# Routed experts of a six-stage kernel: the mask of the two best by replacing them, and the padding cleared behind the router's subtraction

## The chip, the cores and the metric

The kernel runs on one core of a Trainium2 chip. The metric is the device time of one execution in microseconds (us): three runs of the kernel before took 3339.98 to 3342.47 us, with a median of 3340.1. The core's engines work side by side, each through its own queue in order, and meet only at semaphores: TensorE (PE, with its weight load PEld), VectorE (DVE), ScalarE (ACT), GpSimd (POOL), and SyncE (SP), which issues the DMAs here.

## The reference

x has 16 sequences of 256 tokens with 128 channels. Six blocks are added to it one after another. The change touches two of them, the first and the third, which are the same routed FFN with the same weights (the others are a retention layer, two attention-and-expert layers and a plain attention). Cut to the routed FFN:

```python
def _L0_ffn_ref(x, rW1, rb1, rW2, rb2, rW3, rb3, eW1, eb1, eW2, eb2):
    capacity = int(T / E * CAPACITY_FACTOR)                  # 40 slots of each of 8 experts
    h = jax.nn.relu(x @ rW1 + rb1)                           # 128 -> 512
    h = jax.nn.relu(h @ rW2 + rb2)                           # 512 -> 512
    scales = jax.nn.softmax(h @ rW3 + rb3, axis=-1)          # 512 -> 8
    topk_scales, topk_experts = jax.lax.top_k(scales, k)     # the two best of 8
    onehot = jax.nn.one_hot(e_flat, E, dtype=jnp.int32)
    pos_excl = jnp.cumsum(onehot, axis=1) - onehot           # place of a token among its expert's
    keep = pos < capacity
    ...                                                      # tokens to slots, two layers per expert
    out = jnp.sum(topk_scales[..., None] * gathered, axis=2)
x = x + 0.5 * _L0_ffn_ref(_layernorm(x, axis=-1), ...)
```

## The kernel before, in words

`routed_ffn` is called twice. It splits the 32 tiles of 128 tokens into G = 8 groups of GT = 4 tiles, and runs over steps s = 0 to 10. Each engine has its own loop over s, and the order of the work in it is written out by hand. In step s the router works on group s (`layer1`, `layer2`, `partial`, `logits`), the mask, the counting and the slots work on group s - 1 (`count`, `slots`, `turn_weights`), and the experts on an earlier pair of groups (`hidden`, `output`, `turn_slots`, `back`). The engines hand their results over through PSUM banks in four rings of two: `ra` (emptied by ScalarE) and `rv` (emptied by VectorE) for the router, `ea` and `ev` likewise for the experts.

The router's products are made in three parts, of a high and a low part of both factors (`split_product`, L221 to L223). So every h1 chunk goes through two engines: ScalarE (chunks 0 and 2) or VectorE (chunks 1 and 3, `route_hidden`, L573 and L576) takes it from PSUM as high part and as whole, and GpSimd subtracts one from the other for the low part (`rest_of_h1`, L783). TensorE starts layer 2 only when all four low parts are there. The low part of x comes from GpSimd too (L777). The weights' high parts are written by ScalarE (L487), their low parts by VectorE (L689), both in the first FFN only: in the second, `w.load` is None and they are there already.

The experts' slots are found like this, on VectorE: `softmax_divide` (L590 to L596) makes the scores `sc`, 8 for each token; `pick` takes the eight largest in order (`max`, L603) and the places of these (`max_index`, L608) and casts the first two places to float (L611); `mark` compares the numbers 0 to 7 with each of the two (L616), adds the results to the mask (L620), a 1 at the two best experts of each token, and makes an offset of it (L622). `memset(k.idle)` writes a scratch element. TensorE counts with the mask (`count`, L270 and L271), and `place` turns the counts into a 0/1 matrix `d` (L628, L633), which TensorE multiplies with.

Padding: the weighting matrices `gts` and the experts' transposed outputs `eos` fill 80 of the 96 partitions that the products of `back` read, so rows 64 to 95 of four tiles are cleared once at the start of each FFN, by VectorE (L683, each 32 x 2048). Two of these tiles lie in a buffer named all_qs. ScalarE waits for the clears (`padded`) only in step 1, before anything is written to the tiles.

In the profile the names of both FFNs begin with f_: f_ra and f_rv are the router's rings, f_h_hi and f_h_lo the parts of h1, l_rw_hi and l_rw_lo those of the router's weights.

Of the kernel before, what the change touches and what calls it, by code (L numbers as in the profile page):

```python
# [22 lines left out]
U32 = mybir.dt.uint32  # L23
ALU = mybir.AluOpType
# [3 lines left out]
P = 128  # L28
# [4 lines left out]
E0, HID, CAP = 8, 512, 40  # L33
# [4 lines left out]
ROWS = 96  # L38
# [83 lines left out]
def routed_ffn(nc, tag, x_sb, k, w):  # L122

    G, GT, NB = B // 2, 4, 4
# [6 lines left out]
    with ExitStack() as ctx:  # L131
        a = Pool_(nc, ctx, tag)
# [8 lines left out]
        lp = a.sb("lp", [P, W])  # L141
        lg, ex, sc = [a.sb(n, [P, GT, E0]) for n in ("lg", "ex", "sc")]
        top, den = a.sb("top", [P, GT]), a.sb("den", [P, GT])
        best, best_at = a.sb("best", [P, GT, 8]), a.sb("best_at", [P, GT, 8], U32)
        best_f = a.sb("best_f", [P, GT, 2])
        eq = a.sb("eq", [P, GT, 2, E0])
        mask = a.sb("mask", [P, GT, E0], BF16)
        off, pos = a.sb("off", [P, GT, E0]), a.sb("pos", [P, GT, E0])
        d = a.sb("d", [P, GT * E0, CAP])
# [3 lines left out]
        eos, own = a.sb("eos", [ROWS, NB, NW, C]), a.sb("gts", [ROWS, GT, NW, P])  # L153
        stack = [k.qs[:, n, :, :].rearrange("p h t -> p (h t)").bitcast(F32) for n in range(2)]
        gts = [stack[0].rearrange("p (t v c) -> p t v c", t=GT, v=NW), own, stack[1].rearrange("p (t v c) -> p t v c", t=GT, v=NW)]
# [33 lines left out]
        def ring(name):  # L189
# [3 lines left out]

        ra, rv, ea, ev = ring("ra"), ring("rv"), ring("ea"), ring("ev")
        ra_taken, rv_taken, ea_taken, ev_taken = ra.emptied["x"], rv.emptied["h1"], ea.emptied["slots"], ev.emptied["slots"]
        (ln_stats, ln_aggr, ln_veps, ln_rstd, xn_ready, top_ready, lg_ready, ex_ready, den_step, sc_ready, best_step, bestf,
         mask_step, off_ready, d_ready, g_ready, padded, xt_ready, h1_ready, zeroed, ks_zeroed) = [a.sem(n) for n in (
             "ln_stats ln_aggr ln_veps ln_rstd xn_ready top_ready lg_ready ex_ready den_step sc_ready best_step bestf "
             "mask_step off_ready d_ready g_ready padded xt_ready h1_ready zeroed ks_zeroed").split()]
        block = ctx.enter_context(nc.Block())  # L200
        ROUTE = (ra, rv, ra, rv)
# [340 lines left out]
        def _(dve):  # L542
# [15 lines left out]
            def ln_apply(g):  # L558
                dve.wait_ge(ln_rstd, g + 1)
                if g >= 2:  # L560
                    EXPERT[1].full(dve, "slots", (g - 2, 1))
                for t in range(GT):
                    nc.vector.tensor_scalar(xn[:, g % 2, t, :], x_g[:, g, t, :], mv[:, t, 0:1], rstd[:, t:t + 1],
                                            ALU.subtract, ALU.mult).then_inc(xn_ready, 1)
# [34 lines left out]
            def pick(g):  # L599
                dve.wait_ge(sc_ready, g + 1)  # L600
                nc.vector.memset(k.idle, 0.0)
                for t in range(GT):
                    last = nc.vector.max(best[:, t, :], sc[:, t, :])  # L603
                last.then_inc(best_step, 1)
                dve.wait_ge(best_step, g * 2 + 1)
                nc.vector.memset(k.idle, 0.0)
                for t in range(GT):
                    last = nc.vector.max_index(best_at[:, t, :], best[:, t, :], sc[:, t, :])  # L608
                last.then_inc(best_step, 1)
                dve.wait_ge(best_step, g * 2 + 2)  # L610
                nc.vector.tensor_copy(best_f[:, :, :], best_at[:, :, 0:2]).then_inc(bestf, 1)  # L611

            def mark(g):
                dve.wait_ge(bestf, g * 2 + 1)
                for n in range(2):
                    last = nc.vector.tensor_tensor(eq[:, :, n, :], k.iota8.unsqueeze(1).to_broadcast([P, GT, E0]),  # L616
                                                   best_f[:, :, n:n + 1].to_broadcast([P, GT, E0]), ALU.is_equal)
                last.then_inc(bestf, 1)
                dve.wait_ge(bestf, g * 2 + 2)
                nc.vector.tensor_tensor(mask[:, :, :], eq[:, :, 0, :], eq[:, :, 1, :], ALU.add).then_inc(mask_step, 1)  # L620
                dve.wait_ge(mask_step, g + 1)
                nc.vector.tensor_scalar(off[:, :, :], mask[:, :, :], -1000.0, 1000.0, ALU.mult, ALU.add)\  # L622
                    .then_inc(off_ready, 1)
# [45 lines left out]
            def take_slots(q, b):  # L669
                ev.full(dve, "eos", (q, b))  # L670
                nc.vector.tensor_copy(eos[0:SW, b, :, :].rearrange("p v c -> p (v c)"), ev.bank("eos", (q, b))[0:SW, :])\
                    .then_inc(ev_taken, 1)
# [6 lines left out]
            dve.wait_ge(k.loaded, k.loaded_count)  # L679
            ln_measure(0)  # L680
            ln_apply(0)
            for n, tile in enumerate([eos] + gts):
                nc.vector.memset(tile[64:ROWS, :, :, :].rearrange("p b v c -> p (b v c)"), 0.0).then_inc(padded, 1)  # L683
            dve.wait_ge(w.router_loaded, w.router_count)
            if w.load is not None:
                for n, (lo, full, hi) in enumerate(((w.rw1_lo[:, :], w.rw1[:, :], w.rw1_hi[:, :]),
                                                    (w.rw2_lo[:, :, :], w.rw2[:, :, :], w.rw2_hi[:, :, :]))):
                    dve.wait_ge(w.router_hi_ready, n + 1)
                    nc.vector.tensor_tensor(lo, full, hi, ALU.subtract).then_inc(w.router_lo_ready, 1)  # L689
                nc.vector.memset(w.rw3[:, :, E0:32], 0.0)  # L690
                nc.vector.tensor_copy(w.rw3[:, :, 0:E0], w.rw3_in[:, :, :]).then_inc(w.rw3_ready, 1)
            for s in range(G + 3):
                group, q, e = s - 1, (s - 2) // 2, 4 * (s % 2)
                route, given, expert, closed = s < G, 0 <= group < G, 2 <= s < G + 2, s >= 4 and s % 2 == 0
                if route:
                    route_hidden(s, "h1", 1)
                    route_hidden(s, "h1", 3)
                if closed:
                    take_slots(q - 1, 1)
                    take_slots(q - 1, 3)  # L700
                if given:
                    softmax_divide(group)
                    pick(group)
                    mark(group)
                if s % 2:
                    if expert:
                        hidden(q, e)
                        hidden(q, e + 1)
                    if given:
                        place(group)  # L710
                    if s < G - 1:
                        ln_measure(s + 1)
                    if expert:
                        hidden(q, e + 2)
                        hidden(q, e + 3)
                    if route:
                        route_hidden(s, "h2", 1)
                    if given:
                        slots(group)
                    if s < G - 1:  # L720
                        ln_apply(s + 1)
                    if route:
                        route_hidden(s, "h2", 3)
                    if expert:
                        output(q, e // 2 + 1)
                else:
                    if closed:
                        residual(q - 1, 0)
                    if s == G + 2:
                        nc.vector.memset(stack[0][32:64, :], 0.0)  # L730
                    if given:
                        place(group)
                    if s < G - 1:
                        ln_measure(s + 1)
                    if route:
                        route_hidden(s, "h2", 1)
                    if closed:
                        residual(q - 1, 1)
                    if given:
                        slots(group)  # L740
                    if expert:
                        for n in range(4):
                            hidden(q, e + n)
                    if s < G - 1:
                        ln_apply(s + 1)
                    if route:
                        route_hidden(s, "h2", 3)
                    if expert:
                        output(q, e // 2 + 1)
                if given:  # L750
                    take_weights(group, 1)
                    take_weights(group, 3)
                if route:
                    softmax_shift(s)
                if s == 0:
                    dve.wait_ge(w.experts_loaded, w.experts_count)
                    if w.load is not None:
                        w.split_positions(dve)
# [1679 lines left out]
```

## Time and profile before

| what | value |
|---|---|
| median of 3 runs | 3340.1 us |
| the profiled execution | 3345.47 us |
| its span, first to last instruction | 3343.7 us |
| mean granted TensorE clock | 0.949 |
| busy: TensorE, VectorE, ScalarE, GpSimd | 87%, 66%, 59%, 59% |
| first routed FFN | from about 9 us to about 330 us |
| second routed FFN | from about 599 us to about 920 us |

The span is the part of an execution that the profile sees. The two routed FFNs are the stretches with names in f_. A row of a timeline gives a start in us from the span's first instruction, a duration in us, the engine, the line, the operation, what it writes and reads, how many instructions are merged in the row, and in brackets how long the engine was idle before it and what released it. Every row that is used stands in the section on rows below.

### The profile page before, as it was taken

How to read it: one execution, taken by the hardware profiler on the slowest of the kernel's cores; microseconds unless marked ns; L12 is line 12 of the kernel's file. 1: busy time of each engine (PE TensorE's matmuls, PEld its weight loads, DVE VectorE, ACT ScalarE, POOL GpSimd, SP SyncE). 2: the span in 40 equal slices, each digit the busy share in tenths (PEclk: the TensorE clock that was granted, in tenths of full speed). 3: DMA queues.
4: the chain of work that ended last, by engine and by line, in shares of the span. 5: the costliest groups of instructions: out<-in, count | busy, mean ns of one | idle time of the engine just before them, and what ended most of it. 6: DMA issues, size and time to landing. Idle time of an engine off the chain costs nothing. (4 is left out here: it accounts for less than half of the span.)

```text
span 3343.7 us, 68247 instructions
## 1 busy us (share of the span) xinstructions
PE 2921.0 (87%) x21536; PEld 2373.1 (71%) x21536; DVE 2221.2 (66%) x4993; ACT 1969.9 (59%) x5797; POOL 1963.2 (59%) x2223
## 2 busy tenths in 40 slices
PE   6899677699969899997999979995999999979998
PEld 4778555477857777775788856664777777758886
DVE  4544466454459999886555558885888998855554
ACT  2223233222348888886544459995888888844443
POOL 3223554322157777773999942221777777759998
PEclk9999889899979999998999989997999999989999
DMA  3000445000022211122555533331122111145554
GB/s 103 1 1 1 96 108 114 1 1 1 1 47 49 47 38 38 42 49 68 191 191 191 190 89 81 78 77 47 39 50 46 38 38 38 39 149 190 190 191 169
DMA packets 145439, 260.56 MB, mean 78 GB/s; under 512 B 13402, under 2 KB 118106, under 8 KB 122298
## 3 DMA queue, kind: packets, MB, share of 16 engines
q1 hardware_dynamic: 145210, 257.78, 26.7%
q8 instruction: 111, 1.82, 0.2%
q14 instruction: 118, 0.97, 0.1%
HBM read 204.06 MB, written 53.67 MB: 77 GB/s over the span
## 5 line engine op out<-in xcount | busy, mean ns | idle before, releaser
L2223 POOL TENSOR_TENSOR f4m_ht_lo<-f4m_ht,f4m_ht_hi 128x512 fp32r<-128x512 f32 x256 | 330.9, 1311 | 33.3 <-ACT f4m_ht_hi L2168 24.0
L2223 POOL TENSOR_TENSOR f6m_ht_lo<-f6m_ht,f6m_ht_hi 128x512 fp32r<-128x512 f32 x256 | 330.9, 1312 | 33.0 <-ACT f6m_ht_hi L2168 23.7
L2203 DVE SCALAR_TENSOR_TENSOR f4m_ht<-f4m_hr,f4m_gate 128x512 f32<-128x512 f32 x256 | 176.3, 691 | 168.3 <-PE f4m_hr L2099 159.7
L2203 DVE SCALAR_TENSOR_TENSOR f6m_ht<-f6m_hr,f6m_gate 128x512 f32<-128x512 f32 x256 | 176.3, 691 | 167.7 <-PE f6m_hr L2099 160.2
L1711 ACT ACTIVATE f4a_pr<-f4a_sr,f4a_nm 128x256 f32<-128x256 f32 x512 | 239.5, 480 | 60.4 <-DVE f4a_nm L1820 59.0
L2168 ACT ACTIVATE f4m_ht_hi<-f4m_ht 128x512 fp32r<-128x512 f32 x256 | 161.5, 632 | 191.7 <-DVE f4m_ht L2203 191.6
L2168 ACT ACTIVATE f6m_ht_hi<-f6m_ht 128x512 fp32r<-128x512 f32 x256 | 161.5, 632 | 191.5 <-DVE f6m_ht L2203 188.5
L1711 ACT ACTIVATE f6a_pr<-f6a_sr,f6a_nm 128x256 f32<-128x256 f32 x512 | 239.5, 480 | 54.1 <-DVE f6a_nm L1820 52.2
L1956 POOL TENSOR_TENSOR f6a_rr<-f6a_tmp 128x256 f32<-128x256 f32 x256 | 189.0, 738 | 137.2 <-DVE f6a_tmp L1828 136.9
L1956 POOL TENSOR_TENSOR f4a_rr<-f4a_tmp 128x256 f32<-128x256 f32 x256 | 189.1, 739 | 133.5 <-DVE f4a_tmp L1828 133.0
L1711 ACT ACTIVATE a_pr<-a_sr,a_nm 128x256 f32<-128x256 f32 x512 | 252.2, 553 | 10.3 <-DVE a_nm L1820 10.2
L1820 DVE TENSOR_REDUCE a_nm<-a_sr 128x2 f32<-128x512 f32 x256 | 173.4, 684 | 56.6 <-PE a_sr L1568 56.4
L1828 DVE TENSOR_TENSOR f6a_tmp<-f6a_ur,f6a_turn 128x512 f32<-128x512 f32 x256 | 175.2, 685 | 45.2 <-PE f6a_ur L1556 41.2
L1828 DVE TENSOR_TENSOR f4a_tmp<-f4a_ur,f4a_turn 128x512 f32<-128x512 f32 x256 | 175.1, 685 | 44.4 <-PE f4a_ur L1556 40.6
L1962 POOL TENSOR_TENSOR f4a_rr_lo<-f4a_rr,f4a_rr_hi 128x256 fp32r<-128x256 f32 x256 | 192.6, 752 | 1.5 <-ACT f4a_rr_hi L1767 1.5
L1962 POOL TENSOR_TENSOR f6a_rr_lo<-f6a_rr,f6a_rr_hi 128x256 fp32r<-128x256 f32 x256 | 192.5, 752 | 1.5 <-ACT f6a_rr_hi L1767 1.5
L1820 DVE TENSOR_REDUCE f6a_nm<-f6a_sr 128x2 f32<-128x512 f32 x256 | 175.2, 684 | 25.9 <-PE f6a_sr L1574 24.7
L1820 DVE TENSOR_REDUCE f4a_nm<-f4a_sr 128x2 f32<-128x512 f32 x256 | 175.1, 684 | 24.5 <-PE f4a_sr L1574 23.3
L1572 PE MATMUL f6a_sr<-f6a_pe_hi,f6a_rr_hi 128*128 128x256 f32 x512 | 190.2, 371 | 0.0
L1572 PE MATMUL f4a_sr<-f4a_pe_hi,f4a_rr_hi 128*128 128x256 f32 x512 | 189.0, 369 | 0.0
L1696 ACT ACTIVATE f6a_pts<-f6a_tr 128x512 f32<-128x512 f32 x256 | 155.3, 607 | 43.7 <-PE f6a_tr L1584 34.2
L1696 ACT ACTIVATE f4a_pts<-f4a_tr 128x512 f32<-128x512 f32 x256 | 155.5, 607 | 32.3 <-PE f4a_tr L1584 30.4
(423 smaller groups left out, 9905.3 us busy)
## 6 DMA issues: line engine op xcount, KB each, us to landing
f4m_gate<-f4m_gates SPq DMA_DIRECT2D x64, 1024.0 KB, 4.6
f6m_gate<-f6m_gates SPq DMA_DIRECT2D x64, 1024.0 KB, 4.7
r_scratch<-r_parts SPq DMA_DIRECT2D x32, 192.0 KB, 2.2
all_qs<-r_scratch SPq DMA_DIRECT2D x16, 384.0 KB, 4.7
all_ks<-r_scratch SPq DMA_DIRECT2D x16, 384.0 KB, 6.7
f4a_scratch<-f4a_parts SPq DMA_DIRECT2D x32, 192.0 KB, 2.1
all_qs<-f4a_scratch SPq DMA_DIRECT2D x16, 384.0 KB, 5.0
all_ks<-f4a_scratch SPq DMA_DIRECT2D x16, 384.0 KB, 6.7
```

What stands on the lines that cost most here:

```text
L1572: nc.tensor.matmul(out, rr_hi[at], pe_hi[:, :], start=False, stop=False)
L1696: return nc.scalar.activation(dst, src_, ACT.Copy)
L1711: last = nc.scalar.activation(pr[:, n % 4, x, :], sr.bank(b, n)[:, x * T:(x + 1) * T], ACT.Exp, bias=nm[:, n % SB, x:x + 1], accum_out=zs[ ...
L1820: nc.vector.tensor_reduce(nm[:, n % SB, :], sr.bank(b, n).rearrange("p (x s) -> p x s", x=2), AX.X, ALU.max, negate=True).then_inc(nm_read ...
L1828: nc.vector.tensor_tensor(tmp[:, hs % 2, :, :], ur.bank(b, hs).rearrange("p (u t) -> p u t", u=2), turn[:, :, :], ALU.mult).then_inc(ur.em ...
L1956: nc.gpsimd.tensor_tensor(rr[:, hs % RAW, :], tmp[:, hs % 2, 0, :], tmp[:, hs % 2, 1, :], ALU.add)\
L1962: nc.gpsimd.tensor_tensor(rr_lo[:, hs % RRS, :], rr[:, hs % RAW, :], rr_hi[:, hs % RRS, :], ALU.subtract)\
L2168: nc.scalar.activation(ht_hi[:, n % RB, :], ht[:, n % RB, :], ACT.Copy).then_inc(hi_ready, 1)
L2203: nc.vector.scalar_tensor_tensor(ht[:, n % RB, :], hr[:, n % HB, :], 0.0, gate[:, q % GB, n % LOADED, :], ALU.max, ALU.mult).then_inc(ht_r ...
L2223: nc.gpsimd.tensor_tensor(ht_lo[:, n % RB, :], ht[:, n % RB, :], ht_hi[:, n % RB, :], ALU.subtract)\
```

## The change

It has two parts. In `pick`, the eight largest scores stay, but places 2 to 7 of them are overwritten with -1.0, and `match_replace` copies the scores to `left` with the values that match one of the eight replaced by -1.0. Scores are positive, so what is below zero in `left` is one of the two best: `mark` makes the mask by one comparison. The cast, the two comparisons and the addition go, with the tiles `best_at`, `best_f` and `eq` and the semaphore `bestf`; a clear of 6 of 8 elements of `best` comes in, with its wait. In the VectorE queue of each routed FFN, the four clears of padding are moved behind the subtraction of the router's weights and what follows it.

```diff
@@ pick and mark @@
-                dve.wait_ge(best_step, g * 2 + 1)
+                dve.wait_ge(best_step, g * 3 + 1)
+                nc.vector.memset(best[:, :, 2:8], -1.0).then_inc(best_step, 1)
+                dve.wait_ge(best_step, g * 3 + 2)
                 nc.vector.memset(k.idle, 0.0)
                 for t in range(GT):
-                    last = nc.vector.max_index(best_at[:, t, :], best[:, t, :], sc[:, t, :])
+                    last = nc.vector.match_replace(left[:, t, :], best[:, t, :], sc[:, t, :], -1.0)
                 last.then_inc(best_step, 1)
-                dve.wait_ge(best_step, g * 2 + 2)
-                nc.vector.tensor_copy(best_f[:, :, :], best_at[:, :, 0:2]).then_inc(bestf, 1)
 
             def mark(g):
-                dve.wait_ge(bestf, g * 2 + 1)
-                for n in range(2):
-                    last = nc.vector.tensor_tensor(eq[:, :, n, :], k.iota8.unsqueeze(1).to_broadcast([P, GT, E0]),
-                                                   best_f[:, :, n:n + 1].to_broadcast([P, GT, E0]), ALU.is_equal)
-                last.then_inc(bestf, 1)
-                dve.wait_ge(bestf, g * 2 + 2)
-                nc.vector.tensor_tensor(mask[:, :, :], eq[:, :, 0, :], eq[:, :, 1, :], ALU.add).then_inc(mask_step, 1)
+                dve.wait_ge(best_step, g * 3 + 3)
+                nc.vector.tensor_scalar(mask[:, :, :], left[:, :, :], 0.0, None, ALU.is_lt).then_inc(mask_step, 1)
                 dve.wait_ge(mask_step, g + 1)
@@ the start of VectorE's program @@
             ln_measure(0)
             ln_apply(0)
-            for n, tile in enumerate([eos] + gts):
-                nc.vector.memset(tile[64:ROWS, :, :, :].rearrange("p b v c -> p (b v c)"), 0.0).then_inc(padded, 1)
             dve.wait_ge(w.router_loaded, w.router_count)
             if w.load is not None:
...
                 nc.vector.tensor_copy(w.rw3[:, :, 0:E0], w.rw3_in[:, :, :]).then_inc(w.rw3_ready, 1)
+            for n, tile in enumerate([eos] + gts):
+                nc.vector.memset(tile[64:ROWS, :, :, :].rearrange("p b v c -> p (b v c)"), 0.0).then_inc(padded, 1)
```

VectorE's queue at the start of the first FFN, before the change: the layer norm's last part, the four clears, the subtraction, and the evacuations of h1 chunk 1.

```order
10 L563 TENSOR_SCALAR f_xn<-all_x,f_mv,f_rstd 128x128 x4
11 L683 MEMSET f_eos 32x2048
12 L683 MEMSET all_qs 32x2048
13 L683 MEMSET f_gts 32x2048
14 L683 MEMSET all_qs 32x2048
15 L689 TENSOR_TENSOR l_rw_lo<-l_shared,l_rw_hi 128x512
16 L689 TENSOR_TENSOR l_rw_lo<-l_shared,l_rw_hi 128x2048
17 L690 MEMSET l_rw 128x4x24
18 L691 COPY l_rw<-l_rw_in 128x4x8
19 L573 TENSOR_SCALAR f_h_hi<-f_rv,l_rb 128x512
```

The same place of VectorE's queue with the change:

```order
10 L561 TENSOR_SCALAR f_xn<-all_x,f_mv,f_rstd 128x128 x4
11 L680 TENSOR_TENSOR l_rw_lo<-l_shared,l_rw_hi 128x512
12 L680 TENSOR_TENSOR l_rw_lo<-l_shared,l_rw_hi 128x2048
13 L681 MEMSET l_rw 128x4x24
14 L682 COPY l_rw<-l_rw_in 128x4x8
15 L684 MEMSET f_eos 32x2048
16 L684 MEMSET all_qs 32x2048
17 L684 MEMSET f_gts 32x2048
18 L684 MEMSET all_qs 32x2048
19 L571 TENSOR_SCALAR f_h_hi<-f_rv,l_rb 128x512
```

The four clears have moved from ahead of the subtraction to between it and the evacuation. In the second FFN there is no subtraction, and the clears stand where they stood.

VectorE's queue in one group, from the scores to the position (f_pos), before the change:

```order
42 L596 TENSOR_TENSOR f_sc<-f_ex,f_den 128x32
43 L601 MEMSET all_idle 128x1
44 L603 MAX f_best<-f_sc 128x8 x4
45 L606 MEMSET all_idle 128x1
46 L608 MAX_INDEX f_best_at<-f_best,f_sc 128x8 x4
47 L611 CAST f_best_f<-f_best_at 128x8
48 L616 TENSOR_TENSOR f_eq<-all_table,f_best_f 128x4x8 x2
49 L620 TENSOR_TENSOR f_mask<-f_eq 128x32
50 L622 TENSOR_SCALAR f_off<-f_mask 128x32
51 L628 TENSOR_TENSOR f_pos<-f_rv,f_off 128x32
```

The same group with the change:

```order
42 L594 TENSOR_TENSOR f_sc<-f_ex,f_den 128x32
43 L599 MEMSET all_idle 128x1
44 L601 MAX f_best<-f_sc 128x8 x4
45 L604 MEMSET f_best 128x4x6
46 L606 MEMSET all_idle 128x1
47 L608 MATCH_REPLACE f_left<-f_best,f_sc 128x8 x4
48 L613 TENSOR_SCALAR f_mask<-f_left 128x32
49 L615 TENSOR_SCALAR f_off<-f_mask 128x32
50 L621 TENSOR_TENSOR f_pos<-f_rv,f_off 128x32
```

A clear has come in before the matches, and one instruction stands for the cast, the two comparisons and the addition. The other engines' instructions and their order are the same.

## Rows read from the trace of the kernel before

**Rows 1.** The page, busy us and share of the span.

```profile
PE 2921.0 (87%) x21536; PEld 2373.1 (71%) x21536; DVE 2221.2 (66%) x4993; ACT 1969.9 (59%) x5797; POOL 1963.2 (59%) x2223
```

**Rows 2.** Windows: length; busy PE, PEld, DVE, ACT, POOL; PE clock, DMA share, GB/s.

```profile
92.00:122.00 30.00, 29.37 (x180) 24.76 (x178) 14.40 (x40) 11.56 (x27) 7.59 (x7) 1.00 0.01 1
```

**Rows 3.** Waits, 20 to 330 us: total us, times, longest.

```profile
DVE f_pos L628 <- PE f_rv L271: 17.0, 5, 4.9
...
PE f_ra L221 <- POOL f_h_lo L783: 22.3, 8, 4.3
...
PE f_ra L221 <- DVE l_rw_lo L689: 10.5, 1, 10.5
```

**Rows 4.** Timeline of VectorE, start of the first FFN.

```profile
11.57 1.12 DVE L563 TENSOR_SCALAR f_xn<-all_x,f_mv,f_rstd 128x128 f32<-128x128 f32 x4 [1.48 <-POOL f_rstd L766]
...
19.59 1.76 DVE L683 MEMSET all_qs<- 32x2048 f32 x1 [0.38 <-issue]
21.38 2.89 DVE L689 TENSOR_TENSOR l_rw_lo<-l_shared,l_rw_hi 128x512 fp32r<-128x512 f32 x2
...
27.36 0.75 DVE L573 TENSOR_SCALAR f_h_hi<-f_rv,l_rb 128x512 fp32r<-128x512 f32 x1 [2.94 <-PE f_rv L223]
...
40.18 0.75 DVE L576 TENSOR_SCALAR f_h<-f_rv,l_rb 128x512 f32<-128x512 f32 x1 [7.65 <-PE f_rv L223]
```

**Rows 5.** Timelines of ScalarE, GpSimd and TensorE, the same stretch.

```profile
10.71 2.43 ACT L487 ACTIVATE l_rw_hi<-l_shared 128x512 fp32r<-128x512 f32 x2 [0.74 <-DMA l_rb<-in_rb]
...
15.12 1.26 POOL L777 TENSOR_TENSOR f_xt_lo<-f_xt,f_xt_hi 128x512 fp32r<-128x512 f32 x1 [3.59 <-ACT f_xt L433]
...
24.42 0.76 PE L221 MATMUL f_ra<-f_xt_hi,l_rw_hi 128*128 128x512 f32 x1 [10.50 <-DVE l_rw_lo L689]
...
32.73 0.51 PE L221 MATMUL f_ra<-f_h_hi,l_rw_hi 128*128 128x512 f32 x1 [2.85 <-POOL f_h_lo L783]
```

**Rows 6.** Timelines of three engines, start of the second FFN.

```profile
611.72 0.75 DVE L573 TENSOR_SCALAR f_h_hi<-f_rv,l_rb 128x512 fp32r<-128x512 f32 x1
...
624.54 0.75 DVE L576 TENSOR_SCALAR f_h<-f_rv,l_rb 128x512 f32<-128x512 f32 x1 [8.90 <-PE f_rv L223]
...
613.21 3.71 POOL L783 TENSOR_TENSOR f_h_lo<-f_h,f_h_hi 128x512 fp32r<-128x512 f32 x3 [2.06 <-DVE f_h L576]
...
616.97 0.79 PE L221 MATMUL f_ra<-f_h_hi,l_rw_hi 128*128 128x512 f32 x1 [5.45 <-POOL f_h_lo L783]
```

**Rows 7.** Timeline, one group's mask (the third step).

```profile
82.77 4.94 POOL L783 TENSOR_TENSOR f_h_lo<-f_h,f_h_hi 128x512 fp32r<-128x512 f32 x4 [2.42 <-ACT f_h L426]
...
85.33 1.20 DVE L596 TENSOR_TENSOR f_sc<-f_ex,f_den 128x32 f32<-128x32 f32 x1
...
87.67 0.17 DVE L611 CAST f_best_f<-f_best_at 128x8 f32<-128x8 uint32 x1
...
88.42 0.18 DVE L622 TENSOR_SCALAR f_off<-f_mask 128x32 f32<-128x32 bf16 x1
...
92.64 0.19 DVE L628 TENSOR_TENSOR f_pos<-f_rv,f_off 128x32 f32<-128x32 f32 x1 [4.04 <-PE f_rv L271]
```

**Rows 8.** Timelines: a step with experts, and the last group's mask.

```profile
275.81 1.25 DVE L648 TENSOR_SCALAR l_shared<-f_ev,l_eb 128x160 f32<-128x160 f32 x4
...
279.67 0.79 PE L292 MATMUL f_ea<-f_xd,l_ew 128*128 128x160 f32 x4
...
305.41 0.19 DVE L620 TENSOR_TENSOR f_mask<-f_eq 128x32 bf16<-128x32 f32 x1
...
306.13 0.17 PE L271 MATMUL f_rv<-f_mask,all_bf 128*128 128x8 bf16 x1
```

**Rows 9.** Instructions by tile (ns min/median/max), and one group of lines.

```profile
L603 DVE MAX8 f_best<-f_sc x64: 150/152/166, 57.9 to 887.6; 128x8 f32<-128x8 f32 x64
...
L608 DVE FIND_INDEX8 f_best_at<-f_best,f_sc x64: 158/160/165, 58.4 to 888.3; 128x8 uint32<-128x8 f32 x64
...
L690 DVE MEMSET l_rw<- 128x96 f32 x1 | 0.1, 138 | 0.0
```

More of the change, by code:

```diff
@@ L143, in routed_ffn @@
         top, den = a.sb("top", [P, GT]), a.sb("den", [P, GT])
-        best, best_at = a.sb("best", [P, GT, 8]), a.sb("best_at", [P, GT, 8], U32)
-        best_f = a.sb("best_f", [P, GT, 2])
-        eq = a.sb("eq", [P, GT, 2, E0])
+        best, left = a.sb("best", [P, GT, 8]), a.sb("left", [P, GT, E0])
         mask = a.sb("mask", [P, GT, E0], BF16)
@@ L195, in routed_ffn @@
         ra_taken, rv_taken, ea_taken, ev_taken = ra.emptied["x"], rv.emptied["h1"], ea.emptied["slots"], ev.emptied["slots"]
-        (ln_stats, ln_aggr, ln_veps, ln_rstd, xn_ready, top_ready, lg_ready, ex_ready, den_step, sc_ready, best_step, bestf,
+        (ln_stats, ln_aggr, ln_veps, ln_rstd, xn_ready, top_ready, lg_ready, ex_ready, den_step, sc_ready, best_step,
          mask_step, off_ready, d_ready, g_ready, padded, xt_ready, h1_ready, zeroed, ks_zeroed) = [a.sem(n) for n in (
-             "ln_stats ln_aggr ln_veps ln_rstd xn_ready top_ready lg_ready ex_ready den_step sc_ready best_step bestf "
+             "ln_stats ln_aggr ln_veps ln_rstd xn_ready top_ready lg_ready ex_ready den_step sc_ready best_step "
              "mask_step off_ready d_ready g_ready padded xt_ready h1_ready zeroed ks_zeroed").split()]
```

## The prediction

> **What bounds the kernel now.** I read the page's busy shares first: TensorE is busy 87% of the span, with VectorE a good way behind [rows 1]. The change touches only the two routed FFN stages, so the next view was busy time by stretch: in a steady stretch of the first of them, TensorE is busy 29.37 of 30 us, at full clock [rows 2]. Then the waits of that stage. TensorE waits there in three places that matter: eight times before layer 2 of the router, for GpSimd's low parts of h1 (22.3 us together); once, 10.5 us long, for VectorE's low parts of the router's weights, right at the start; and hardly elsewhere. The third row says the reverse of what a saving in the mask would need: VectorE waits for TensorE's count (17.0 us in five waits) just after it has made the mask [rows 3]. So the mask has time to spare, and the start has not. The rest of the reading is timelines of the start and of one mask.
>
> **Part 1, the padding at the start of the first FFN.** Today VectorE ends the layer norm of group 0 at 11.57 + 1.12 = 12.69 us, clears four tiles one after another, the last from 19.59 to 19.59 + 1.76 = 21.35, and only then subtracts the router's weights, from 21.38 for 2.89 us; a small clear and a copy follow until 24.42. TensorE's first layer-1 product starts at 24.42, released by that subtraction [rows 4, 5]. Nothing the subtraction needs is that late: ScalarE has written both high parts by 10.71 + 2.43 = 13.14, and had waited for the weights' DMA until 10.71 [rows 5]. The change swaps two blocks on one in-order queue: clearing (12.69 to 21.38, 8.7 us with its gaps) and subtraction with its two small followers (21.38 to 24.42, 3.04 us). Afterwards the subtraction runs 12.7 to 15.6 and TensorE can start layer 1 when GpSimd's low part of x is ready, which is at 15.12 + 1.26 = 16.4 us [rows 5]: 8.0 us earlier.
>
> Not all of that arrives. The four clears now stand between the subtraction and VectorE's two evacuations of h1 (chunks 1 and 3). The two blocks keep their sum, so VectorE comes free at 24.4, as today. Today it then idles until the first chunk is there and starts at 27.36 [rows 4]; afterwards chunks 1 and 3 have been in PSUM since about 16.4 + 5.5 = 21.9 at the latest (today's layer 1 takes from 24.42 to 32.73 - 2.85 = 29.88 [rows 5]), and VectorE starts at 24.4. That is 2.96 us earlier. What follows this is on the path: VectorE evacuates, GpSimd takes the low parts of chunks 1, 2, 3, and TensorE starts layer 2. The second routed FFN already shows this very pattern, because its weights are already split and its clears already stand right ahead of the evacuations: TensorE has ended layer 1 at 616.97 - 5.45 = 611.52, VectorE starts evacuating only at 611.72, GpSimd follows at 613.21 for 3.71 us, and layer 2 starts at 616.97 after those idle 5.45 us [rows 6]. From evacuation to layer 2 is 616.97 - 611.72 = 5.25 us. So layer 2 of group 0 starts at 24.4 + 5.25 = 29.65 instead of 32.73 [rows 5]: 3.1 us earlier, and a wait of about 8 us for GpSimd's low parts takes the place of today's 2.85.
>
> The idle stretch before layer 2 grows, and the clock may answer. Today the first matmul of layer 2 lasts 0.51 us [rows 5]; in the second FFN, after 5.45 us idle, 0.79 [rows 6]. The sum of layer 2 hardly differs: VectorE's next evacuation starts 7.45 us after layer 2's start in the first FFN (40.18) and 7.57 us after it in the second (624.54) [rows 4, 6]. I take 0.1 us off: the start gives **3.0 us**. Bounds: if the clears hid altogether, 8.0 us; if a clear took longer beside the weights' DMAs, less, but they lie beside those DMAs today too. In the second FFN the order of instructions is the same before and after, so nothing comes from there.
>
> **Part 2, the mask, in 16 groups (8 in each FFN).** Before: four max, four match-and-index pairs, a cast, two compares, an add, then the offset. From the cast to the offset it is 88.42 - 87.67 = 0.75 us [rows 7]. Afterwards the cast, both compares and the add (0.75 us) are gone; one tensor_scalar (0.18, as the offset's) with a handoff of 0.04 comes in their place; a clear of 24 elements with a handoff comes ahead of the matches. A clear of 96 elements takes 0.138 us [rows 9]; I take 0.10 for this one and 0.04 for the handoff. The trace has no match-and-replace. The nearest rows are MAX8 with 0.152 and FIND_INDEX8 with 0.160 us [rows 9]; both read the same tile of 8 elements, so I take 0.16 and leave the four pairs as they are. Below: 4 x 0.05 less. Above: one that waits for GpSimd as the multiply at 85.33 does (1.20 us, where GpSimd's four subtractions run from 82.77 to 87.71) [rows 7]. The chain becomes 0.75 - 0.22 - 0.14 = 0.39 us shorter, from 0.6 shorter to, with one such wait, 0.4 longer.
>
> On the path this counts for nothing. In the step of rows 7 the mask ends before 88.42 and the count is done only just before 92.64: VectorE's wait grows from 4.0 to 4.4 us. In a step with experts, VectorE's evacuations of hidden stand behind the mask; they run from 275.81 for 1.25 us, and TensorE wants their banks back from 279.67, over 2.6 us later [rows 8]. The tightest place is the last group, where no layer 2 covers the mask: the mask starts at 305.41 and is there at 305.60, TensorE comes to the count at 306.13 after its products of the fourth group before [rows 8]. It is still 0.5 us early. So part 2 is 16 x 0.39 = 6.2 us less work on VectorE and 0 us of time; the cover is TensorE's layer 2, and without it the cost or gain would be these 6.2 us.
>
> **Sum.** 3.0 + 0 = 3.0 us. The profiled execution took 3345.47 us (span 3343.7 and 1.8 around it), so it would take 3342.5; it lay 5.4 above the median of 3340.1, which I carry over: **3337.1 us**, 0.09% less. This is less than the 0.2% (6.7 us) that counts as a change here.
>
> **A rule weighed.** The multiply at 85.33 has 32 elements per partition and lasts 1.20 us, against 0.19 for the offset-sum at 92.64 of the same size; it ends at 86.53, where the third of GpSimd's four subtractions ends (82.77 + 3/4 of 4.94 = 86.5) [rows 7]. The Trainium skill (SBUF — State Buffer, Who interferes with whom) says that a VectorE instruction with two inputs in SBUF and a GpSimd instruction that reads SBUF exclude each other for the whole instruction, and that tensor_scalar may take a mode that does so too. By that rule the trace agrees. It speaks against the change at one place: the long subtraction now runs until 15.6, across GpSimd's start at 15.12, so that x's low part would come 0.5 us later. By it the start of layer 1 would gain 7.5 instead of 8.0 us, and the sum would stay at 3.0, since VectorE at 24.4 decides.
>
> **Rivals.**
> A. The clears hide: layer 2 doesn't wait for them. Gain about 8 us, 3332 us. For it: TensorE's start does move by 8 us. Against: the clears stand in an in-order queue ahead of what layer 2 needs, and rows 6 show TensorE idle for just this. 0.04.
> B. The mask is on the path after all, in each group: 3.0 + 6.2 = 9.2 us, 3330.9. Against: VectorE waits 17.0 us for the count [rows 3]. 0.04.
> C. GpSimd pays. The new tensor_scalar gets in ahead of GpSimd's fourth subtraction, for which TensorE waits before layer 2, and pushes it by 0.22 us in 14 steps (seven in each FFN): 3.1 us back, 3340.2. By rows 7 it starts near 87.8, after GpSimd's end at 87.71, so it is just too late for that. 0.08.
> D. Slower: match-and-replace costs as much as the waiting multiply, 1.20 us in place of 0.16, all four times. The chain grows by 4 x 1.04 - 0.39 = 3.8 us. The steps with the 4.0 us of room of rows 7 absorb it, the last group with its 0.5 does not: 3.3 us in each FFN, 6.6 - 3.0 = 3.6 us more, 3343.7; beyond 1.2 us each, every step pays and it passes 3350. It decides from 0.38 us each on, where 4 x 0.22 - 0.39 uses up the 0.5 us of the last group. Against: the two neighbours with 0.15 and 0.16. 0.04.
> E. The start gives nothing, because a later fixed point (a load, the clock in the next steps) takes the 3 us back: 3340. The waits show no DMA that TensorE waits for in this stage. 0.08.
>
> **How the numbers follow.** The forecast has 0.72, with 3335 to 3339 as its own range. Range for 8 in 10: the forecast, C and E lie within 3333.5 to 3341.0. Faster by over 0.2% (below 3333.4): A, B and a little for what I don't see, 0.09. Slower by over 0.2% (above 3346.8): the far end of D and the unseen, 0.03. Same: 0.88.
>
> **What would show it.** In the new profile: TensorE's first router product at 16.4 to 17.0 us; VectorE's four clears from about 16 to 24.4; its first evacuation at 24.4; layer 2 at 29.6 to 29.8, after an idle stretch of about 8 us for GpSimd; the second FFN's start with its 5.45 us idle unchanged, and the length of a step of the router unchanged. The mask chain from the multiply's end to the offset's start 1.5 us instead of 1.9, with VectorE's wait for the count longer by the difference. It would be wrong if layer 2 starts before 28 us, or if the distance from it to the end of the first FFN changes by more than 1 us, or if TensorE waits anywhere for the mask.

## The result and the profile after

| kernel | median us | lowest to highest, runs |
|---|---|---|
| before | 3340.4 | 3337.1 to 3342.5, 6 |
| changed | 3357.4 | 3352.9 to 3361.3, 6 |

The ratio is 1.005, with a 95% interval of 1.0038 to 1.0062. The forecast was 3337.1, a little faster; the change costs 17 us. The profiled execution of the changed kernel took 3361.3 us, with a span of 3359.6, 15.9 more than before.

The page first, engine by engine, as in [rows 1]:

```profile
PE 2926.6 (87%) x21536; PEld 2377.4 (71%) x21536; DVE 2212.7 (66%) x4961; ACT 1968.3 (59%) x5797; POOL 1960.6 (58%) x2223
```

VectorE executes 32 instructions fewer and is busy 8.5 us less, near the 6.2 that the prediction takes off it. So the loss is no busy time. Where each stage starts in the two traces tells more (us, changed minus before): retention −3.3, the fourth stage's attention (f4a) +3.3, its expert part +18.9. The first routed FFN gains about what it should. Retention and the second FFN lose some us in code that the change leaves alone or moves by nothing; retention took between 245 and 253 us in the ten profiled runs, so that loss is its scatter. Then 15.6 us are lost in one stage, f4a, of which no line is changed. Its waits, the changed kernel (us in total, times, longest):

```profile
ACT f4a_pr L1704 <- DVE f4a_nm L1813: 73.5, 93, 4.1
...
DVE f4a_tmp L1821 <- issue: 14.5, 5, 2.9
...
PE f4a_ur L1549 <- DVE f4a_tmp L1821: 13.5, 5, 2.8
```

The same waits in the kernel before (its L1828 is L1821 after):

```profile
ACT f4a_pr L1711 <- DVE f4a_nm L1820: 59.0, 85, 1.6
...
DVE f4a_tmp L1828 <- issue: 2.0, 5, 0.4
...
PE f4a_ur L1556 <- DVE f4a_tmp L1828: 1.0, 5, 0.3
```

"Issue" is a wait for nothing that the profile shows: no semaphore, no other engine. It comes five times, and f4a's middle part is a hardware loop (`Fori` in `steps`), which VectorE runs six times, so with five jumps back; one pass has 276 records of VectorE in the trace, semaphore and register instructions included. Every pass but the first begins with that wait. One of the five jumps back, the second, before and then changed (VectorE's timeline):

```profile
1184.30 0.23 DVE L1870 TENSOR_TENSOR f_gates<-f4a_pick 128x64 f32 x1
1184.93 0.69 DVE L1828 TENSOR_TENSOR f4a_tmp<-f4a_ur,f4a_turn 128x512 f32<-128x512 f32 x1 [0.40 <-issue]
```

```profile
1190.93 0.23 DVE L1863 TENSOR_TENSOR f_gates<-f4a_pick 128x64 f32 x1
1194.02 0.69 DVE L1821 TENSOR_TENSOR f4a_tmp<-f4a_ur,f4a_turn 128x512 f32<-128x512 f32 x1 [2.86 <-issue]
```

What VectorE may wait for at a jump is the code itself; the experiments below are on that. The DMA view for 1170 to 1490 us (four jumps in either kernel), changed:

```profile
q1 hardware_dynamic: 14168, 13.05, 18.5%
q14 instruction: 20, 0.16, 0.2%
```

and before, where the row of q14 is missing:

```profile
q1 hardware_dynamic: 14080, 12.59, 17.9%
```

q14 carries instructions. Before, it brings nothing in this stretch of the loop; with the change it brings 20 packets of some 8 KB, 5 for each of the four jumps. The other thing that differs in the loop is the clock, here in the first 10 us of a pass (windows; us, busy PE, PEld, DVE, ACT, POOL, clock, DMA share, GB/s), before and changed:

```profile
1184.40:1194.40 10.00, 8.32 (x78) 6.79 (x77) 8.26 (x15) 7.52 (x28) 8.34 (x11) 1.00 0.00 0
```

```profile
1191.00:1201.00 10.00, 6.08 (x34) 4.98 (x32) 5.97 (x11) 4.75 (x17) 4.77 (x7) 0.66 0.01 2
```

All engines stand still together, since VectorE is what the others wait for, and behind the stall TensorE works part of the time at the lower of its two clocks (granted 0.66 on the mean: 0.51 to 0.52 from 1194 to 1201 us, 1.00 ahead of that and from 1201 on). The stall is 2.5 us longer than before; the pass as a whole is 3.4 us longer ((393.0 − 375.9) / 5, from the table at the end of the next section), so some 0.9 us are what follows from the stall.

### The profile page after: what moved, and what is told of

Read it like the earlier page. It is cut to its first block and busy times, and to the rows that moved or that the text cites. A ratio compares the mean times of both kernels' runs of the same rounds, so it can differ in the third digit from the quotient of the medians.

```text
span 3359.6 us, 68214 instructions
## 1 busy us (share of the span) xinstructions
PE 2926.6 (87%) x21536; PEld 2377.4 (71%) x21536; DVE 2212.7 (66%) x4961; ACT 1968.3 (59%) x5797; POOL 1960.6 (58%) x2223
## 5 line engine op out<-in xcount | busy, mean ns | idle before, releaser
L1821 DVE TENSOR_TENSOR f4a_tmp<-f4a_ur,f4a_turn 128x512 f32<-128x512 f32 x256 | 174.9, 684 | 59.2 <-PE f4a_ur L1549 37.9
L1821 DVE TENSOR_TENSOR f6a_tmp<-f6a_ur,f6a_turn 128x512 f32<-128x512 f32 x256 | 174.9, 684 | 46.2 <-PE f6a_ur L1549 42.4
```

The lines of the kernel that those rows point to most:

```text
L1821: nc.vector.tensor_tensor(tmp[:, hs % 2, :, :], ur.bank(b, hs).rearrange("p (u t) -> p u t", u=2), turn[:, :, :], ALU.mult).then_inc(ur.em ...
```

## The experiments

The theory after the traces was: **place**. The loop's code is read again in every pass or stays with the engine, and which of the two it is depends on where the loop begins in VectorE's program. The change made the program ahead of f4a's loop 33 instructions shorter: VectorE has 2127 records ahead of the second pass instead of 2160. Of these, 32 are the mask's (two in each of 16 groups), and one that isn't counted as busy goes with the clears' move. The rival: an instruction of the new mask, or the moved clears, costs something that reaches f4a in another way. The table at the end of this section has both loops of every run.

**1. The clears' move alone** (the mask as before):

```diff
-            for n, tile in enumerate([eos] + gts):
-                nc.vector.memset(tile[64:ROWS, ...], 0.0).then_inc(padded, 1)
             ...                                      # subtraction, clear, copy of the router's weights
+            for n, tile in enumerate([eos] + gts):
+                nc.vector.memset(tile[64:ROWS, ...], 0.0).then_inc(padded, 1)
```

> The kernel before with only the clears moved; VectorE's program keeps its length. Place theory (the loop of the fourth stage is slow because VectorE's program is 33 instructions shorter ahead of it, and its code is read anew in each pass): the loop is as before, 5 passes of about 75.1 us with 0.4 us idle at their start, q14 with about 118 packets; gain 2.4 to 3 us at the start, 3337 us. Rival (moving the clears disturbs the later stages): about 3357 us.

Measured: 3340.4 us beside 3341.3 of before, ratio 0.9999 (0.9989 to 1.0008). No loss, but the expected 3337 didn't come either: the gain is smaller than what the comparison can tell. The program doesn't quite keep its length, as the expectation says: it is one instruction shorter ahead of the loop.

**2. The mask alone** (the clears as before):

```diff
-                    last = nc.vector.max_index(best_at[:, t, :], best[:, t, :], sc[:, t, :])
+                    last = nc.vector.match_replace(left[:, t, :], best[:, t, :], sc[:, t, :], -1.0)
...
+                nc.vector.tensor_scalar(mask[:, :, :], left[:, :, :], 0.0, None, ALU.is_lt).then_inc(mask_step, 1)
```

> The kernel before with only the mask by match-and-replace; the program is 33 instructions shorter. Place theory: passes of 78.7 us with 2.9 us idle, q14 with about 144 packets, +17 us without the 2.4 us of the start: 3357 to 3360 us. Rival (the clears are to blame): 3340 us.

Measured: 3359.1, ratio 1.0059 (1.0042 to 1.0076). The whole loss comes with the mask, but this doesn't tell its instructions from its length (32 instructions shorter by the trace, not 33).

**3. The change, and 33 instructions back.** In VectorE's wait for the count of group 1 of the second FFN:

```diff
             def place(g):
...
+                if w.load is None:
+                    for n in range({1: 34}.get(g, 0)):
+                        nc.vector.memset(pads[:, 34 * g - 34 + n:34 * g - 33 + n], 0.0)
```

> The changed kernel with 33 more VectorE instructions in the second routed FFN: 34 clears of one element each, in the wait for the count of group 1, where VectorE is idle for over 4 us. Nothing of the change is undone. Place theory: the length ahead of the loop is that of before, so passes of 75.1 us, q14 near 118 packets, 3337 us. Rival (the new instructions or the tiles' new places in memory are to blame): 3357 us, or more by the clears.

Measured: 3341.2, ratio 1.0 (0.9991 to 1.001). The change with all its instructions is as fast as before, once 34 useless ones (33 net) are added. This is what the rival can't give.

**4. The kernel before, made 95 instructions longer.** The same clears in the waits of groups 1 to 3, nothing of the change:

```diff
+                if w.load is None:
+                    for n in range({1: 34, 2: 34, 3: 27}.get(g, 0)):
+                        nc.vector.memset(pads[:, ...], 0.0)
```

> The kernel before with 95 more VectorE instructions in the waits for the count of groups 1 to 3 of the second routed FFN (one-element clears of 0.06 us). 95 is 128 - 33, and a q14 packet of 8192 bytes would hold 128 instructions of 64 bytes. Place theory: the loop lies as in the changed kernel with respect to these blocks, so passes of 78.7 us, q14 near 145 packets, 3357 us, with nothing of the change in it. Rival (only a shorter program, new instructions or new tiles slow it): 3340 us.

Measured: 3359.9, ratio 1.006 (1.0043 to 1.0077). The loss appears without the change. Its place lies exactly 128 instructions behind the changed kernel's, so a longer program is no protection, and the slow place has come back after 128, as the expectation had it.

**5. The change and 16 instructions back** (17 clears, 16 net, at the place of experiment 3):

```diff
-                    for n in range({1: 34}.get(g, 0)):
+                    for n in range({1: 17}.get(g, 0)):
```

> The change with 17 one-element clears on VectorE (16 instructions net, half as many as in the run before that won the time back), in the wait for the count of group 1 of the second routed FFN. It asks whether length alone or the place decides. Place theory: what matters is where the instructions of a loop begin, modulo a fixed stretch of code. The loop of the fourth stage (f4a, 5 passes) then begins 16 instructions further, which should take it out of the bad stretch (passes back to about 75.1 us, 0.4 us idle at their start), but the loop of the sixth stage (f6a), which begins a little over 100 instructions later, should get into the bad stretch: its passes grow by about 3.5 us each, with an idle time of about 2.9 us at the start of each pass of VectorE, some 25 more code reads of 8192 bytes there, and the total stays about 3357. Rival 1, the number of instructions ahead of f4a alone has a threshold: either both loops are fine and it is 3341, or f4a is still slow and it is 3357 with f6a as before. Rival 2, every instruction fewer costs in proportion: half of 17, 3349.

Measured: 3362.3, ratio 1.0061 (1.0043 to 1.0078). The total alone looks like the threshold rival, "f4a still slow". The waits of VectorE say otherwise, first from 2250 to 2970 us (the sixth stage), then from 932 to 1600:

```profile
DVE f6a_tmp L1825 <- issue: 14.8, 5, 3.1
```

```profile
DVE f4a_tmp L1825 <- issue: 2.0, 5, 0.5
```

The loss has moved from the loop of f4a to the loop of f6a, the same code in the sixth stage, as the place theory says. It is larger than expected there: 22 us by the table, not 17.5.

**6. The change, and 33 instructions behind the loop.** The program is as long as before, the loop lies where the change put it:

```diff
+            if tag == "f4m":
+                for n in range(33):
+                    nc.vector.memset(pads[:, n:n + 1], 0.0)
```

> The change with 33 one-element clears at the start of VectorE's program for the expert part of the fourth stage (f4m), behind the loop of f4a, where VectorE waits some 6 us for ScalarE anyway. The program is as long as before, but what lies ahead of f4a's loop is as short as in the change. Place theory: f4a's passes stay at 78.6 us with 2.9 us idle at their start, total about 3357; f6a as before. Rival, the length of the whole program counts (or where a later stage lies): back to 3341.

Measured: 3357.6, ratio 1.0043 (1.0028 to 1.0058), f4a's waits on issue 14.7 us in five. The total length doesn't count, what lies ahead of the loop does.

**7. The kernel before with the clears later.** The prediction says that the clears ahead of the evacuations hold layer 2. Here they stand in step 0 behind the second group's layer-norm measure, where VectorE waits 8 us for layer 2 anyway ([rows 4]: 7.65):

```diff
+                    if s == 0:
+                        for n, tile in enumerate([eos] + gts):
+                            nc.vector.memset(tile[64:ROWS, ...], 0.0).then_inc(padded, 1)
```

> The kernel before, with the four clears of padding behind the second group's layer-norm measure in step 0, where VectorE idles 7.6 to 8.9 us for TensorE's layer 2; VectorE's program is as long as before. If the clears ahead of the evacuations are all that held the start (my step of the prediction): in the first FFN the subtraction runs 12.7 to 15.6, layer 1 starts at about 16.7, the evacuations start at about 19.7, layer 2 at about 25 instead of 32.7 (7.5 us), in the second FFN layer 2 of group 0 comes 1 to 2 us earlier; the total is 6 to 9 us shorter, 3332 to 3335. Rival 1, the half clock after the idle start takes part of it: 3 to 5 us, 3336 to 3338. Rival 2, a later fixed point takes it all back: 3341.

Measured: 3332.9 us beside 3343.6 of before, ratio 0.9965 (0.9953 to 0.9977). VectorE and GpSimd, and TensorE's layer 2, in this run:

```profile
16.03 1.13 DVE L689 COPY l_rw<-l_rw_in 128x32 f32<-128x32 f32 x1
20.14 0.75 DVE L573 TENSOR_SCALAR f_h_hi<-f_rv,l_rb 128x512 fp32r<-128x512 f32 x1 [2.98 <-PE f_rv L223]
...
25.79 1.76 DVE L735 MEMSET f_eos<- 32x2048 f32 x1 [0.48 <-issue]
```

```profile
25.51 0.49 PE L221 MATMUL f_ra<-f_h_hi,l_rw_hi 128*128 128x512 f32 x1 [2.85 <-POOL f_h_lo L784]
```

Layer 2 starts at 25.5 instead of 32.73 [rows 5], with the same 2.85 us idle ahead of it, and the clears, from 25.79 on, lie under it. In the second FFN the distance from layer 1's start to layer 2's goes from 616.97 − 606.83 = 10.1 us to 8.3 (604.25 to 612.59).

**8. The same with the new mask**, and 34 clears that keep the loop at its place: the candidate that beats both kernels.

> The change's mask, with 34 one-element clears as padding of code (the place of f4a's loop one instruction from where it was before) and the clears of padding in step 0 behind the second group's layer-norm measure, as in the run with late clears alone. The mask costs and gives nothing by both theories, so it should equal that run within 0.1%: 3332 to 3335, with f4a's passes at 75.1 us. It is the candidate that beats both kernels. If the new mask were worth its 6 us of VectorE time, it would be 6 us below that run.

Measured: 3332.4 (3328.0 to 3334.9), ratio 0.9965 (0.9951 to 0.9979). It beats both, but by no more than experiment 7, which has the old mask. So the new mask is worth nothing that this comparison can tell, and the gain is that of the clears.

All runs in one table, from the profiled executions. "Place" is the number of VectorE instructions ahead of f4a's loop against before, counted by the trace's records; the loops' times are those of the last five of six passes together, from the first jump back to the loop's end; q14 is the number of its packets in f4a and in f6a (925 to 1570, 2300 to 2965 us); "first r_xn" is the start of retention, so the end of the first FFN.

| kernel | place | first r_xn | f4a loop | f6a loop | q14 in f4a, f6a |
|---|---|---|---|---|---|
| before | 0 | 348.7 | 378.8 | 379.5 | 16, 41 |
| changed | −33 | 345.4 | 393.0 | 375.9 | 41, 43 |
| 1 clears only | −1 | 347.7 | 375.9 | 375.8 | 17, 41 |
| 2 mask only | −32 | 349.5 | 393.0 | 375.8 | 41, 43 |
| 3 changed, +33 | 0 | 347.5 | 375.9 | 376.3 | 16, 41 |
| 4 before, +95 | +95 | 349.5 | 393.6 | 375.6 | 41, 43 |
| 5 changed, +16 | −17 | 347.2 | 375.9 | 398.1 | 17, 66 |
| 6 changed, 33 behind | −33 | 347.6 | 393.2 | 379.3 | 41, 42 |
| 7 late clears | 0 | 341.4 | 376.0 | 376.3 | 17, 41 |
| 8 both, late clears | +1 | 341.9 | 376.1 | 376.5 | 17, 41 |

f4a's five passes take 376 us or 393. The 378.8 of before has one pass of 78.5 among four of 75.1 on the mean, and f6a's loop took 379.5 and 379.3 in two runs; both without the stall, so some 3.5 us of scatter are another matter, of unknown cause. f4a's loop is slow in the four runs at −33, −32 and +95 and in no other, and f6a's in the one at −17, where it costs more: 398.1 − 376, 4.4 us a pass. Why one loop is slow where the other is not is their distance: from the start of f4a's to the start of f6a's the program has 1516 instructions with a record, which is 12 × 128 − 20. So f6a's place at −17 answers to about −37 of f4a's, and its fast places to about −20 and −53 (estimates, a few too low if some instructions leave no record).

## Why the prediction was wrong

**The step that failed is the sum.** "3.0 + 0 = 3.0 us" took its terms from the two FFNs, and carried the profiled time of all else over unchanged. What an instruction costs was asked of each removed and added one; what their number does to the code behind them wasn't asked of any, and so stood at nothing without a reason. The change takes 33 instructions out ahead of two loops. For f4a's that is a term of its own, 393.0 − 375.9 = 17.1 us (375.9 is the loop in experiments 1, 3 and 5; against the 378.8 of the one profile of before it is 14.2), and it is the whole result: 17.1 for the loop and −2.1 for the start (below) make 15.0, within the measured interval of 0.38 to 0.62% (12.7 to 20.7 us). It was missing among the rivals too; the 0.03 for slower by over 0.2% was held by the far end of D and by what the prediction calls the unseen. The profile of before had a hint: each of f4a's and f6a's passes starts with 0.4 us of VectorE on "issue" (2.0 us in five), so there is a cost at that jump, and its page lists 118 packets on q14. It has no row with the stall itself, so its size could only have been had from a run.

**Part 1, the start: the mechanism was right, the size too large (3.0 us said, 2.1 measured).** The changed kernel's VectorE, as in [rows 4]:

```profile
12.59 2.88 DVE L680 TENSOR_TENSOR l_rw_lo<-l_shared,l_rw_hi 128x512 fp32r<-128x512 f32 x2
15.44 0.14 DVE L681 MEMSET l_rw<- 128x96 f32 x1
15.50 1.13 DVE L682 COPY l_rw<-l_rw_in 128x32 f32<-128x32 f32 x1
...
23.53 1.76 DVE L684 MEMSET all_qs<- 32x2048 f32 x1 [0.38 <-issue]
25.33 0.75 DVE L571 TENSOR_SCALAR f_h_hi<-f_rv,l_rb 128x512 fp32r<-128x512 f32 x1
```

TensorE, as in [rows 5], and GpSimd's low part of x:

```profile
16.65 0.79 PE L219 MATMUL f_ra<-f_xt_hi,l_rw_hi 128*128 128x512 f32 x1 [2.74 <-POOL f_xt_lo L770]
30.57 0.79 PE L219 MATMUL f_ra<-f_h_hi,l_rw_hi 128*128 128x512 f32 x1 [9.39 <-POOL f_h_lo L776]
```

```profile
15.10 1.49 POOL L770 TENSOR_TENSOR f_xt_lo<-f_xt,f_xt_hi 128x512 fp32r<-128x512 f32 x1 [3.58 <-ACT f_xt L431]
19.67 1.28 POOL L776 TENSOR_TENSOR f_h_lo<-f_h,f_h_hi 128x512 fp32r<-128x512 f32 x1 [3.08 <-ACT f_h L424]
```

The copy of the router's last weights in the kernel before, a row of the timeline of [rows 4]:

```profile
24.30 0.12 DVE L691 COPY l_rw<-l_rw_in 128x32 f32<-128x32 f32 x1
```

Layer 1 starts at 16.65 (said: 16.4 to 17.0), and the four clears stand between the copy and the evacuation, as said. The evacuation starts at 25.33 instead of 24.4, layer 2 at 30.57 instead of 29.65, with 5.24 us between them (said: 5.25). The 0.9 us come from one row: the copy of 32 elements takes 1.13 us instead of 0.12, and ends at 16.6 with GpSimd's instruction (15.10 + 1.49). The weighed rule of the Trainium skill (SBUF — State Buffer, Who interferes with whom) did speak of this overlap, and names copy among the instructions that can be shut out; I applied it to the subtraction's end only, and put the price on GpSimd. The row agrees with the rule, and puts most of the price on the copy behind the subtraction, which before stood clear of GpSimd. In the four other kernels with this start the copy takes 1.13 us too, and the evacuation starts at 25.5 to 25.6. Layer 2 starts on the mean at 30.76 in these five kernels and at 32.65 in the three with the old start, so 1.9 us earlier and not 3.1. The first FFN ends on the mean at 349.2 with the old start (three runs) and at 347.1 with the new one (five runs, 345.4 to 347.7): 2.1 us, not 3.0. So what arrives at layer 2 arrives at the end. From 25 to 45 us the granted clock is 0.91 before and 0.79 with the change (0.74 in experiment 1), behind the 9.39 us of idle, but no loss from it shows: from layer 2's start to the end of the first FFN it is 316.0 us before and 314.8 with the change. These 1.2 us are over the 1 us that the prediction named as a sign of being wrong, but the four other kernels with this start have 316.3 to 316.9, the two others with the old start 316.9. In the second FFN the start is unchanged, as said: 10.14 us from layer 1 to layer 2 in both kernels. Rival A is excluded by layer 2's start at 30.57, and experiment 7 shows the reason: only with the clears behind the evacuations do the 8 us arrive (7.6 in the first FFN: 349.2 − 341.6).

**Part 2, the mask: its own instructions cost no time, as said; their number is the term above.** One group, the changed kernel, as in [rows 7]:

```profile
82.10 1.20 DVE L594 TENSOR_TENSOR f_sc<-f_ex,f_den 128x32 f32<-128x32 f32 x1
...
83.78 0.08 DVE L604 MEMSET f_best<- 128x24 f32 x1
...
84.57 0.18 DVE L613 TENSOR_SCALAR f_mask<-f_left 128x32 bf16<-128x32 f32 x1
84.78 0.18 DVE L615 TENSOR_SCALAR f_off<-f_mask 128x32 f32<-128x32 bf16 x1
89.39 0.19 DVE L621 TENSOR_TENSOR f_pos<-f_rv,f_off 128x32 f32<-128x32 f32 x1 [4.43 <-PE f_rv L269]
```

By tile (ns min/median/max):

```profile
L608 DVE MATCH_VALUE_LOAD f_left<-f_best,f_sc x64: 79/81/86, 54.1 to 891.8; 128x8 f32 x64
L608 DVE MATCH_REPLACE8 f_left<-f_best,f_sc x64: 149/151/154, 54.2 to 891.8; 128x8 f32<-128x8 f32 x64
L613 DVE TENSOR_SCALAR f_mask<-f_left x16: 181/182/1144, 54.8 to 892.0; 128x32 bf16<-128x32 f32 x16
```

From the multiply's end (83.30) to the offset (84.78) it is 1.48 us (said: 1.5; before 1.89), and VectorE's wait for the count grows from 4.04 to 4.43, by just that difference. Match-and-replace lasts 0.151 us beside the 0.16 that I took, so rival D is out. B is out too: experiment 3, with mask and clears but the old place, is at 1.0 of before, not 9 us below. C didn't happen in this group: the new instruction starts at 84.57, just behind the end of GpSimd's four subtractions (79.53 + 4.94 = 84.47), as said. It can have happened as an exception (one of the mask's 16 instructions reaches 1.144 us, none in experiment 3), and no cost of it shows.

**Rival E**, the start's gain taken back by the time of the end, stays open. The 2.1 us are there at the end of the first FFN, but not seen in the total: experiments 1 and 3 took 3340.4 and 3341.2 beside 3341.3, where E says no difference and 2.1 us less would be 3339.2: their intervals (−3.7 to +2.7 us, −3.0 to +3.3) hold both. For the larger gain of experiment 7 E doesn't hold: 0.23 to 0.47% of the total, 8 to 16 us, beside the 7.6 + 1.8 us of the two starts.

## What to carry to other kernels

Where an edit adds or removes instructions ahead of a hardware loop, in the queue of the engine that bounds the loop, the loop's first row in each pass ("issue" in brackets) and the packets of the instruction queue within it belong in every comparison of two profiles, before any reasoning on the edit itself. A loss in a stage that wasn't touched, in equal portions per pass and with a longer "issue" at each jump, was a matter of place here: pad it by a few dozen cheap instructions in a wait, and judge the edit only then. And clears that nobody needs yet belong into a wait of their engine, behind the instructions that somebody waits for, not merely behind the first of them.

## What the runs showed of the hardware

- A loop of 276 VectorE instructions ran in 75.1 us per pass at four places (−17, −1, 0, +1), and in 78.6 with 25 packets more on q14 in five passes at three others (−33, −32, +95). The slow places −33 and +95 are 128 instructions apart; 118 packets carried 0.97 MB, so 8.2 KB each. That the code comes in pieces of 128 instructions, and that the loop touches one piece more at the slow places than stay with the engine, is a reading that fits all ten runs, but is not shown by itself: only these seven places were tried for f4a's loop; the bounds of the bad stretch and the number of pieces kept weren't measured.
- The Trainium skill (Runtime: NRT & Kernel Launch, Instruction fetch mechanics) says that a taken branch to code outside what the engine holds must fetch it before it goes on, and the rows agree: 2.9 us instead of 0.4 at each jump back, with packets on q14. It gives pieces of 256 instructions, two of which are held. An estimate by that page: 276 instructions touch three pieces of 256 instead of two at 19 of 256 places that lie side by side, and two places 128 apart, like −33 and +95, can't both be among them. The measurement decides against pieces of 256 here, and packets of 8.2 KB speak for half that size.
- Packets alone are no stall. In f6a q14 brings 41 packets also in the kernels whose passes take 75 us and start with 0.4 us; the slow case has 66. For which code the 41 are is not shown.
- A copy of 128 x 32 elements took 1.13 us beside a GpSimd instruction (1.13 and 1.14 in experiments 7 and 8 too) and 0.12 without one (before), while clears of 32 x 2048 took 1.76 us with or without GpSimd at work (GpSimd's row at 19.67, 1.28 us long, lies over one of them).
